# Four constant products of TensorE ahead of every group's scores in the softmax loop

## What is computed

```python
attn = jnp.einsum("bhnd,bhmd->bhnm", q, k) * attn_scale
attn, s_attn = fq_act(attn)              # 8 bits, scale from the min and max of all scores
attn = int_log_softmax(attn, s_attn)     # x/s - max, quotient and remainder, weights, powers of two
o = jnp.einsum("bhnm,bhmd->bhnd", attn, v)
```

## Time and profile before

| what | value |
|---|---|
| median of 3 runs | 1145.65 us (1141.47 to 1145.91) |
| the profiled execution | 1140.23 us, its span 1138.1 us |
| mean granted TensorE clock | 0.725 of full speed |
| softmax loop | from about 434 to 652 us of the span |

### The profile page before, as it was taken

One profiled execution on the slowest core, in us unless ns is written; L12 is line 12 of the kernel. 1 busy time (PEld: TensorE's weight loads), 2 busy tenths in 40 slices (PEclk: granted clock), 3 DMA queues, 4 the chain that ended last, 5 costly groups with the idle time before them and its releaser, 6 DMA issues.

```text
span 1138.1 us, 25696 instructions
## 1 busy us (share of the span) xinstructions
PE 797.2 (70%) x8714; PEld 612.1 (54%) x8714; DVE 807.4 (71%) x1718; ACT 498.7 (44%) x1014; POOL 400.6 (35%) x381
## 2 busy tenths in 40 slices
PE   3898990557437744899999604204379999999998
PEld 2897990446324522556556401003357777777777
DVE  3324432789959996888888476896747777777776
ACT  2122210334374232777777720402245555555554
POOL 1120000478412101222222104270046666666665
PEclk9898995677755555555555555555579999999999
DMA  7642302100012211222222170000000000000000
GB/s 185 169 125 79 96 29 79 55 1 0 0 46 75 77 28 37 36 38 43 37 43 42 13 209 19 0 0 10 1 16 24 23 30 22 21 29 14 29 22 21
DMA packets 112974, 51.84 MB, mean 46 GB/s; under 512 B 75896, under 2 KB 107808, under 8 KB 112928
## 3 DMA queue, kind: packets, MB, share of 16 engines
q1 hardware_dynamic: 111600, 44.94, 16.3%
q0 software_dynamic: 1328, 6.30, 2.0%
HBM read 26.47 MB, written 6.68 MB: 29 GB/s over the span
## 4 chain that ended last, share of the span: by engine, by line
PE 51%; DVE 19%; issue 9%; ACT 8%; SPq 5%; DMA 4%; POOL 2%; DVEq 1%; ACTq 0%; POOLq 0%
PE ps L1258 43%; ACT R L607 5%; PE ps L1417 4%; DMA R<-h_rows 2%; SPq L437 2%; DVE M L999 2%; DVE M L998 2%; ACT ps L706 2%; DVE R L1173 1%; PE ps L1329 1%; SPq L475 1%; ACT R L610 1%; DVE R L1079 1%; DVE R L988 1%; DVE R L1182 1%
## 5 line engine op out<-in xcount | busy, mean ns | idle before, releaser
L1258 PE MATMUL ps<-R 128*128 128x192 f16 (+9 forms) x3788 | 468.0, 276 | 28.1 <-DVE R L843 12.8
L1258 PEld LDWEIGHTS ps<-R 128*128 128x128 f16 (+5 forms) x3788 | 357.9, 114 | 115.2 <-issue 55.6
L599 POOL TENSOR_TENSOR R<-R 128x256 f32<-128x256 f32 x238 | 196.0, 831 | 174.0 <-DVE R L1235 172.0
L1258 PE MATMUL ps<-M 32*64 32x68 bf16 (+2 forms) x2048 | 124.6, 248 | 70.5 <-DMA M<-R 52.5
L1235 DVE TENSOR_TENSOR R<-R,ps 64x256 f32<-64x256 f32 (+1 forms) x272 | 113.9, 419 | 62.2 <-ACT R L786 41.2
L786 ACT ACTIVATE R<-ps 128x256 f32<-128x256 f32 x238 | 91.3, 384 | 135.9 <-PE ps L1258 128.8
L1258 PEld LDWEIGHTS ps<-M 32*64 32x64 bf16 (+2 forms) x2048 | 82.5, 133 | 126.0 <-issue 69.3
L607 ACT ACTIVATE R<-R 128x256 f16<-128x256 f32 (+5 forms) x264 | 118.7, 451 | 33.5 <-POOL R L532 21.7
L607 ACT ACTIVATE R<-ps 68x896 bf16<-68x896 bf16 (+6 forms) x123 | 81.0, 661 | 112.5 <-PE ps L1329 53.2
L1242 DVE TENSOR_TENSOR R<-R 128x256 f16<-128x256 f32 x238 | 113.3, 477 | 20.1 <-ACT R L607 18.0
L610 ACT ACTIVATE R<-R,sc 128x512 f16 (+11 forms) x71 | 65.6, 990 | 114.8 <-POOL R L549 41.6
(11 more groups left out here) (220 smaller groups left out, 1062.9 us busy)
## 6 DMA issues: line engine op xcount, KB each, us to landing
R<-in_x_dram SPq DMA_DIRECT2D x12, 576.0 KB, 7.9
M<-R SPq DMA_DIRECT2D x16, 260.0 KB, 2.4
M<-R SPq DMA_DIRECT2D x32, 130.0 KB, 2.1
R<-h_rows SPq DMA_DIRECT2D x4, 816.0 KB
R<-h_rows SPq DMA_DIRECT2D x1, 3264.0 KB, 12.9
R<-R SPq DMA_DIRECT2D x17, 192.0 KB, 2.5
out_dram<-R SPq DMA_DIRECT2D x17, 192.0 KB, 2.0
M<-R SPq DMA_DIRECT2D x128, 12.8 KB
```

Source lines behind the costliest of these rows:

```text
L599: pool.tensor_tensor(hs[0:rows, m % HB, :], hr[0:rows, m % HB, :], other, ALU.mult).then_inc(sem("squared"), 1)
L1258: return pe.matmul(o, a, b, start=start, stop=stop, skip_group_check=True)
```

## The change

Ahead of every group's scores in the softmax loop, PE makes four more products. Each has `ident_h` as weights (all 128 rows and 128 columns of the array) and the first 240 columns of `wqT0` as the moving operand. They write columns 272 to 511 of banks 0 to 3, one product to a bank. Nobody reads the results. They stand behind the two waits of `second_scores`.

```diff
@@ -1395,6 +1395,8 @@
             def second_scores(g, par, half):
                 pe.wait_ge(sem(f"st_qk{par}"), (8 + half + 1) * 48)
                 wait(pe, "dist", g)
+                for bank in range(4):
+                    mm(ps[:, bank, 4 * N:512], ident_h, wqT0[:, 0:512 - 4 * N])
                 scores(g, 0, par, 0)
```

## The result

| kernel | median | lowest to highest | profiled execution |
|---|---|---|---|
| before | 1143.56 us (4 runs) | 1138.66 to 1145.91 | 1140.23 us |
| changed | 1161.12 us (4 runs) | 1155.48 to 1167.0 | 1161.16 us |

The ratio is 1.016, with a 95% interval of 1.0097 to 1.0223: the change makes the kernel slower, by 17.6 us in the medians. The forecast was 19.0 us slower, 1164.6 us. The profiled executions differ by 20.9 us.

A forecast was written before the change was run, and what follows sets the result against it. Not one engine but a circle of PE, ACT and DVE waiting for each other was the bound. 28 x (6.82 - 6.255) = 15.8, with 3.2 for early steps, gave +19.0: 1145.65 + 19.0 = 1164.6 us, range 1147 to 1171.

The forecast's parts named there:

- The four products: Price of the products added ahead of the scores: 0.80 us a group at half clock, 0.43 at full clock.
- rival C: Weights loads of the added products show: 1.35 us a group, +37 us, 1182 us; chance 0.04.
- The group at half clock: One softmax-loop group at half clock goes from 6.33 to 6.97 us, since 0.64 of 0.80 lies on the path.
- today's rise: In the kernel before, one full-clock stretch among six loop groups, taken to save 0.45 us.
- the second turning's wait of 0.16: PE's wait for ACT's first copy before the second turning, taken as room for 0.16 of the added 0.80 us.
- The early steps: First four loop steps, without turnings: distances wait for the scores directly, so the full 0.80 counts, 3.2 us in all.
- What the clock gives back: In the loop, one clock rise in three groups, 0.45 us each, takes 0.15 off the mean group, giving 6.82.
- What is late next: DVE's wait moves from the weights to the distances; ACT's wait before its second copy goes from 0.61 to about 1.2.
- Rival A: Added products keep the loop's clock full, DVE bounds at about 5.76 us a group: -15 us, 1130 us; chance 0.16.
- Rival B: Clock full in half to three quarters of loop groups, 6.36 to 6.06 us each: 1143 to 1152 us; chance 0.12.
- The level: Starting time for the whole kernel: the median of the runs shown, 1145.65 us, 5.4 above the profiled execution.

The follow-up runs named there:

- 8 + 4: Eight added products ahead of the scores and four ahead of the second turning in each group, against the kernel before: ratio 1.0071.

## Why the prediction was right, and where it wasn't

**The four products** cost what was forecast, 0.80 at half clock by the scores' start behind the remainders. The weights loads didn't show (rival C): no idle time stands ahead of the added products. The spacing by columns is also what the Trainium skill (TensorE: Matmul & The Clock Gate, Part 1) gives for the slow clock, 240 columns / 1.2 GHz = 0.20 us, and the trace agrees.

**The group at half clock** was sized too low: forecast 6.97, and some 7.05 by the runs (7.18 - 0.13 on the quarter of the array, 6.83 + 0.21 by the scores). The change itself has 6.97, 6.96 and 7.13 ahead of its first rise. The starting value hid it. The forecast took 6.33 for every group at half clock before, but they are 6.33 and 6.26 us long in turn. With the distances at 518.75 these are the next two starts:

```profile
525.08 1.32 DVE L1079 SCALAR_TENSOR_TENSOR R<-ps,sc,M 128x544 f16<-128x544 f32 x2
...
531.34 1.32 DVE L1079 SCALAR_TENSOR_TENSOR R<-ps,sc,M 128x544 f16<-128x544 f32 x2
```

So six would take 37.77 and not 37.98, and today's rise saves 0.24 and not 0.45. Of the 0.80, some 0.75 lies on the path (7.05 - 6.295), not 0.64: the forecast subtracted the second turning's wait of 0.16 as room, and the runs leave 0.05.

**The early steps** cost 0.67 each, not the full 0.80. The step that failed is the one that let the distances wait for the scores directly. They stood behind DVE's weights, without an idle time in the earlier trace rows, and that bracket's absence was to be read. It is a room of 0.13, 0.5 us in all.

**What the clock gives back** was sized too low as well: 0.15 a group forecast, some 0.21 measured. One rise in three groups, worth 0.45, was the forecast. Measured were one rise in nearly every group, worth 0.2, in one execution, and one in two groups, worth 0.4, in the other. So 7.05 - 0.21 was measured and 6.97 - 0.15 forecast. That the sum comes out at 6.84 and 6.82 is luck: two errors of 0.06 to 0.08 cancel. The 0.45 came from the reading of six equal groups above; what a rise gave in the changed kernel is what it took off the scores, 0.2 or 0.4. The forecast clock of 0.55 to 0.65 missed the first profile (0.73) and held the second (0.62). By the measured distances the sum is 28 x (6.843 - 6.245) = 16.7, with 4 x 0.67 = 2.7 makes 19.4, against the 19.0 forecast.

**What is late next.** The forecast had DVE wait ahead of the distances instead of ahead of the weights. It waits ahead of both, 0.49 to 0.70 and 0.5. The squares still come late for DVE since the remainders start late, held by the quotients. ACT's wait for the second turning was to go up to 1.2: it is 1.18 where the turning runs at half clock (488.56) and 0.64 where it runs full (549.73).

The changed kernel's group at half clock shows this:

```profile
485.75 1.99 PE L1258 MATMUL ps<-M 32*64 32x68 bf16 x32
...
487.68 0.85 PE L1419 MATMUL ps<-ident_b,R 128*68 128x128 bf16 x6
487.91 1.33 DVE L1079 SCALAR_TENSOR_TENSOR R<-ps,sc,M 128x544 f16<-128x544 f32 x2 [0.70 <-PE ps L1258]
...
488.56 0.81 ACT L607 ACTIVATE R<-ps 68x768 bf16<-68x768 bf16 x1 [1.18 <-PE ps L1419]
```

**Rival A** was the right one to fear, at the wrong dose. Four products in one place don't hold the clock; twelve in two places did in one profile from the sixth step on, and fifteen did in most groups. Its price was near: 5.93 a group measured, 5.76 forecast, so 0.31 gained where 0.49 was forecast, with DVE as the bound. What the forecast's A lacked is the way there and back: neither the early steps nor the last ones may pay. **Rival B**, up and down, is what happened to the clock, but not to the time, since it priced each group with a rise as if it ran at full clock from end to end. The chances were added up with a slip: with a third of B, as the text says, slower would be 0.75 and the same 0.09; 0.77 and 0.07 take half of it.

**The level.** The forecast was set on the median shown, 1145.65; the four runs of before give 1143.56. So 1164.6 against 1161.12 is 3.5 too high, of which 2.1 is the level and 1.4 the difference (19.0 against 17.6, well inside the interval of 11 to 26 us).

**Open.** The profiled executions differ by 20.9, and 1.5 of it lies outside the sum, in the stages ahead of the loop and behind it, which differ between executions of any kernel here. Whether the clock counts the turnings isn't settled by the earlier trace rows: every group has both, and the clock rose in one of six. Open too is why the clock rises once a group in one execution and once in two in another, of the same kernel; and why it holds with 8 + 4 in one profile, yet falls in another of the same loop behind other early steps. The number of products, the share of the array and the place each went with a different clock, and the runs don't make a rule of it. Products behind the scores in every step, into banks 0 to 3, where DVE reads the scores at that time, weren't tried.

## What to carry to other kernels

Before pricing a change of clock, ask which circle each stretch of full clock will fall on: a mean clock of 0.73 or 0.62 was worth 0.2 us in 7.05, what it took off the scores, and one of 0.59 was worth 0.28 where the circle ran through the turnings. Before multiplying one group's length, look whether the groups are alike: here they were long and short in turn. Constant products that wait their turn on the path cost their columns at the slow clock, from the first on; what held the clock here stood in two or three places of the step. Steps at the start and at the end of a pipeline, without half of its work, need their own fill or none, or they pay the price: 7.1 us at the start and 1.5 at the end, against 8.1 gained, with 8 + 4. Count them before hoping for a gain; here no profiled loop came out more than 0.4 us ahead of before.

## What the runs showed of the hardware

- With four products of 240 columns a group the clock was 0.73 and 0.62 on the whole array and 0.56 on a quarter of it (0.55 without any), though PE's busy time was higher there, 113.33 of 120 us. The Trainium skill (TensorE: Matmul & The Clock Gate, Part 1) says that sustained activity releases the clock; with PE's busy time as the measure of activity these rows don't agree.
- Eight and four whole-array products in two places gave a clock of 1.00 from 510 to 630 us. Twelve in one place, in one of the two long executions of that kernel, gave 0.70, in a cycle of four groups with distances from 6.32 to 8.56 us.
- Two executions of one kernel settled into different patterns, a full stretch in nearly each group or in every second (0.73 and 0.62), with the same time: the scores took 1.78 and 1.80 us, or 1.59 and 1.99 in turn.
